# Routing of the first mixture layer: transposes ahead of time, choices taken on logits, and one scatter per choice

## The chip, the cores and the metric

The kernel runs on one core of a Trainium2 chip. The metric is the device time of one execution in microseconds (us), as the median of several executions. Engines are named as the profile names them: PE is TensorE, with PEld for its weight loads, DVE is VectorE, ACT is ScalarE, POOL is GpSimd, and SP is SyncE, which here only issues DMAs.

## The reference, cut to what matters

The program is a decoder of four layers on x of shape (8, 256, 128), float32. Each layer has a self-attention, a cross-attention and a feed-forward part, each followed by a residual sum and a layernorm. The change touches the feed-forward part of layer 0, a mixture of 8 experts, and the last steps of the cross-attention ahead of it.

```python
E, TOP_K, D, H, CAPACITY = 8, 2, 128, 512, 256
xf = x.reshape(b * s, d)                      # 2048 tokens of 128
logits = xf @ Wg                              # 2048 x 8
probs = softmax(logits, axis=-1)
vals, idx = top_k(probs, TOP_K)
w = vals / (sum(vals, -1, keepdims=True) + 1e-09)
for k in range(TOP_K):
    oh = one_hot(idx[:, k], E)
    pos = cumsum(oh, axis=0) - 1 + counts[None, :]
    keep = (oh == 1) & (pos < CAPACITY)
    counts = counts + sum(keep, axis=0)       # the second choice queues behind the first
    combine = combine + w[:, k][:, None] * keep
for e in range(E):
    h = gelu(xf @ W1[e] + b1[e])
    out = out + combine[:, e][:, None] * (h @ W2[e] + b2[e])
```

Each token goes to its two best experts, each expert takes at most 256 (token, choice) pairs in order, all first choices ahead of all second choices, and what does not fit is dropped.

## The kernel before, in words

The stages run in the order L0a, L0x, L0f, L1a and so on: the cross-attention L0x is followed by the mixture L0f. Every engine has its own program, written out by hand, and the engines meet in semaphores. `sem.wait_ge(n)` holds an engine, and with it all that stands behind it in its program. Nothing is reordered at run time. x lies in SBUF as `x_tok`, 16 tiles of 128 tokens (two tiles per batch), and the semaphore `x_done` counts batches that have gone through a stage's layernorm.

**The end of L0x.** The stage is a loop over steps g, with 8 steps (PAIRS) per batch. The last scores are computed at g = 63 and the last weighted values at g = 65. For the last batch there follow the copy of the outputs by VectorE (L2401), their turning by TensorE (L1273), the division by VectorE (L2412 to L2418), a transpose (L1289), a copy by ScalarE (L1964), the output projection (L1297), and residual, moments and normalisation by VectorE (L2473, L2242 to L2253), with the inverse root of the variance by GpSimd in between (L630).

**The routing in L0f.** TensorE waits until all eight batches are normalised, transposes the 16 tiles (L1380) into four PSUM banks, and after ScalarE's copies to `QT` (L2015) forms 16 products of 128 tokens by 8 logits (L1386). VectorE subtracts each token's largest logit (L2619, L2620), ScalarE takes the exponentials (L2017), and VectorE works out probabilities and both choices as one-hot rows (`top2`, L2579 to L2589; `w8` holds 8 for expert 0 down to 1 for expert 7 and breaks ties). Four small TensorE products with a triangle and with ones give positions within a tile and counts per tile for both choices (L1394, L1396). VectorE sums the counts over the tiles in four doubling steps (L2632, L2634) and turns choice and position into a row number of a DRAM buffer `x_slots` (8 experts of 256 rows), `slot_of`, for both choices at once (L2638 to L2662). A token that is not kept gets a number beyond the bound, which the DMA skips.

GpSimd fills some constants at the start of L0f (`later_consts`, L615 to L625). Then it waits for `slot_of` and issues 32 indirect DMAs (L804), one per tile and choice, each writing 128 rows of `x_tok` into `x_slots`. SyncE waits for all 32 to land and loads the buffer back (L584). TensorE, ScalarE and VectorE run the experts from there (L1404 to L1425, L2023, L2670, L2674), their results go to `y_slots` (L588), and GpSimd fetches two rows per token with 32 more indirect DMAs (L795) that VectorE weighs and adds (L2687, L2691).

TensorE waits for `later_consts` ahead of the first expert's input. Of these constants the experts read only `SEL`, in L1425.

## Time and profile before

| | us |
|---|---|
| median of 3 runs (2016.09 to 2019.49) | 2016.48 |
| the profiled execution, its own time | 2024.31 |
| its span in the trace | 2022.6 |
| routing, from the first transpose to the first scatter | 298.16 to 323.13 |
| 32 scatters, first start to last start | 323.13 to 363.05 |
| experts, first to last TensorE instruction | 368.33 to about 410 |
| 32 fetches and the final sums | 413.30 to about 465 |

Starts in the trace count from the start of the span. The profiled execution took 7.8 us more than the median of the others. Its own parts are compared with each other. The granted clock of TensorE is given as a share of full speed, 2.4 GHz, so that 0.50 is 1.2 GHz.

### The profile page before, as it was taken

Reading aid. Unit: us, or ns where it says so; the run is one execution under the profiler, and the core shown is the slowest. Engines: PE = TensorE matmul, PEld = TensorE weight load, DVE = VectorE, ACT = ScalarE, POOL = GpSimd, SP = SyncE. Lnnn points to the kernel's source line nnn. Section 1 sums busy time; section 2 is a strip of 40 time slices with the busy share of each in tenths; the row PEclk is TensorE's granted clock in tenths of the full one; section 3 lists DMA queues with packets and bytes.
Section 4 is the critical chain, followed back from the end, with each engine's and each line's share of the span. In section 5 each row is a group of like instructions: output and inputs, shape, how many; then the busy total and the mean of one; then the engine's idle time right before and its main releaser. Section 6 shows DMA issues by size and latency. Waiting matters only on the chain.

```text
span 2022.6 us, 34313 instructions
## 1 busy us (share of the span) xinstructions
PE 1636.8 (81%) x12460; PEld 1173.2 (58%) x12460; DVE 1373.1 (68%) x3111; ACT 1096.4 (54%) x2271; POOL 697.5 (34%) x773
## 2 busy tenths in 40 slices
PE   6588871737999788879898889988989987888864
PEld 5344431625777655567777767765559964555532
DVE  2577752137777699567999767759964456478876
ACT  4488850205777477538788345546764441147642
POOL 1344434167888302234665512220000020001238
PEclk9699975868999999986887899999999998979985
DMA  2200000110000000010000100000000000000000
GB/s 89 101 12 11 6 33 36 41 36 18 2 1 1 1 1 2 4 37 1 1 1 1 58 1 2 2 11 1 2 1 1 1 17 1 16 1 1 2 1 21
DMA packets 10422, 29.26 MB, mean 14 GB/s; under 512 B 2113, under 2 KB 6663, under 8 KB 9361
## 3 DMA queue, kind: packets, MB, share of 16 engines
q1 hardware_dynamic: 8210, 24.98, 3.5%
q0 software_dynamic: 2048, 2.12, 0.4%
q8 instruction: 101, 1.65, 0.3%
q14 instruction: 63, 0.52, 0.1%
HBM read 23.92 MB, written 5.24 MB: 14 GB/s over the span
## 4 chain that ended last, share of the span: by engine, by line
PE 41%; DVE 19%; POOL 13%; issue 8%; ACT 3%; DMA 0%; POOLq 0%; DVEq 0%; ACTq 0%
PE PS L1117 5%; PE PS L1199 4%; DVE negmax L2370 4%; PE PS L1259 3%; POOL big L738 3%; PE PS L1454 3%; PE PS L1465 3%; DVE V L2864 3%; POOL big L726 2%; POOL big L734 2%; PE PS L1700 2%; PE PS L1281 2%; DVE QS L2430 1%; PE PS L1174 1%; PE PS L1616 1%
## 5 line engine op out<-in xcount | busy, mean ns | idle before, releaser
L1900 ACT ACTIVATE big<-PS 128x1024 f32<-128x1024 f32 (+1 forms) x256 | 248.2, 971 | 135.8 <-PE PS L1210 135.2
L2370 DVE TENSOR_REDUCE negmax<-PS 128x4 f32<-128x1024 f32 x192 | 234.5, 1222 | 46.2 <-PE PS L1199 44.2
L630 POOL TENSOR_TENSOR rstd<-veps,mhalf 128x2 f32<-128x2 f32 x80 | 58.1, 726 | 397.9 <-DVE veps L2248 396.7
L1199 PE MATMUL PS<-KS,QS 32*128 32x256 f32 (+1 forms) x1152 | 134.8, 320 | 48.2 <-DVE negmax L2370 41.9
L1199 PEld LDWEIGHTS PS<-KS,QS 32*128 32x128 f32 x1152 | 86.5, 188 | 124.5 <-DVE negmax L2370 88.5
L1259 PE MATMUL PS<-big,V 128*32 128x256 f32 (+1 forms) x2048 | 134.4, 381 | 0.0
L1210 PE MATMUL PS<-QS,KS 32*128 32x256 f32 (+1 forms) x1152 | 133.1, 318 | 1.4 <-ACT big L1900 1.4
L1956 ACT ACTIVATE KS<-PS,NB,W 128x256 fp32r<-128x256 f32 x160 | 81.6, 561 | 78.3 <-PE PS L1117 49.2
L656 POOL TENSOR_TENSOR res<-resb,XB 128x256 f32<-128x256 f32 x24 | 17.4, 727 | 303.9 <-ACT resb L1970 303.9
L1956 ACT ACTIVATE QS<-PS,NB,W 128x256 fp32r<-128x256 f32 x160 | 81.6, 561 | 40.7 <-PE PS L1117 40.7
L1117 PE MATMUL PS<-xT,W 128*128 128x256 f32 x320 | 90.4, 407 | 13.3 <-ACT xT L1939 11.3
L692 POOL TENSOR_SCALAR KT<-QT 128x1024 f32<-128x1024 f32 x64 | 66.7, 1042 | 90.4 <-DVE QT L2389 71.6
L952 PE MATMUL PS<-OT,W 128*128 128x256 f32 x272 | 74.9, 397 | 26.3 <-ACT QT L1859 26.3
L2389 DVE SCALAR_TENSOR_TENSOR QT<-PS,wint 128x1024 f32<-128x1024 f32 x64 | 77.5, 1220 | 24.3 <-PE PS L1152 24.0
L1255 PE MATMUL PS<-big,V 128*32 128x512 f32 x512 | 72.8, 693 | 24.4 <-ACT big L1922 12.9
L2430 DVE SCALAR_TENSOR_TENSOR QS<-PS,W,QS 128x256 fp32r<-128x256 f32 x160 | 69.6, 477 | 33.6 <-ACT QS L1956 33.5
L1616 PE MATMUL PS<-On,V 128*128 128x128 f32 x512 | 89.2, 347 | 0.0
L2430 DVE SCALAR_TENSOR_TENSOR KS<-PS,W,KS 128x256 fp32r<-128x256 f32 x160 | 69.5, 476 | 28.3 <-ACT KS L1956 28.2
L1616 PEld LDWEIGHTS PS<-On,V 128*128 128x128 f32 x512 | 82.9, 254 | 9.9 <-issue 9.9
L1210 PEld LDWEIGHTS PS<-QS,KS 32*128 32x128 f32 x1152 | 84.2, 186 | 5.8 <-issue 4.0
L2038 ACT ACTIVATE QT<-PS,W 128x256 f32<-128x256 f32 x128 | 53.7, 471 | 60.0 <-PE PS L1454 60.0
L1600 PE MATMUL PS<-OT,SEL 16*128 16x256 f32 x256 | 74.3, 436 | 13.7 <-DVE V L2868 13.6
(412 smaller groups left out, 4530.5 us busy)
## 6 DMA issues: line engine op xcount, KB each, us to landing
W<-in_wpack SPq DMA_DIRECT2D x1, 4180.0 KB, 13.6
W<-in_wpack SPq DMA_DIRECT2D x1, 2836.5 KB, 9.2
W<-in_wpack SPq DMA_DIRECT2D x1, 2560.0 KB, 8.6
W<-in_wpack SPq DMA_DIRECT2D x3, 772.0 KB, 5.2
mask_i<-in_mask SPq DMA_DIRECT2D x8, 256.0 KB, 2.7
W<-in_wpack SPq DMA_DIRECT2D x1, 1798.0 KB, 6.9
x_tok<-in_x SPq DMA_DIRECT2D x1, 1024.0 KB, 4.9
ctxT<-in_ctx SPq DMA_DIRECT2D x1, 1024.0 KB, 7.7
```

The costliest lines, as they stand in the source:

```text
L952: mm = nc.tensor.matmul(PS[:, QKB[u % 2], k * S:(k + 1) * S], w(f"{n}_w{x}", h * P, (h + 1) * P), OT[:, b, :], start=True, stop=True)
L1117: mm = nc.tensor.matmul(o, w(f"{n}_spread" if a.rope else f"{n}_w{x}", (t0 + t) * P, (t0 + t + 1) * P), rhs, start=True, stop=not masked)
L1199: mm = nc.tensor.matmul(PS[:, MAXB[half], o], QS[r, bm % 2, tm, j * P:(j + 1) * P], KS[r, bm % 2, tm, k], start=not a.causal, stop=last)
L1210: mm = nc.tensor.matmul(PS[:, exp_banks(ge)[half], o], KS[r, be % 2, te, kb * P:(kb + 1) * P], QS[r, be % 2, te, q], start=not a.causal, s ...
L1259: mm = nc.tensor.matmul(out_rows[:, skip:S], v, PX[:, T % 2, h, kb * S:(kb + 1) * S - skip], start=first, stop=last)
L1600: mm = nc.tensor.matmul(PS[:, CB + k // 2, (k % 2) * S:(k % 2 + 1) * S], SEL[:, 4 * c + k, :], C_rows(b), start=True, stop=True)
L1616: mm = nc.tensor.matmul(PS[:, YB, j * P:(j + 1) * P], chunk("h", t)[:, at:at + P], by_state[:, 4 * c + k, :], start=False, stop=c == 3 and ...
L1900: nc.scalar.activation(PX[:, T % 2, 2 * p:2 * p + 2, 0:cols], PS[:, exp_banks(g)[0]:exp_banks(g)[0] + 2, 0:cols], ACT.Exp, scale=a.scale). ...
L1956: ins = nc.scalar.activation(dst[:, b % 2, t0 + t, :], PS[:, bank, t * S:(t + 1) * S], ACT.Identity, bias=NB[:, "qk".index(x), t0 + t:t0 + ...
L2370: ins = nc.vector.tensor_reduce(negmax[:, h:h + 2, :].rearrange("p h j -> p (h j)"), banks.rearrange("p h (j k) -> p (h j) k", j=2), AX.X, ...
L2389: nc.vector.scalar_tensor_tensor(clipped(QT, g), PS[:, pair_banks(g):pair_banks(g) + 2, :], -100.0 / a.scale, capT[:, g // PAIRS % 2, :].u ...
L2430: ins = nc.vector.scalar_tensor_tensor(to, PS[:, bank, t * S:(t + 1) * S], w(f"{n}_b{x}", t0 + t, t0 + t + 1), to.bitcast(F32), ALU.add, A ...
```

## The change

The first 14 of the 16 transposes move into the last steps of L0x, between instructions of the last batch, and ScalarE's copies with them. The bank of each tile is `logit_bank(t)`. The last two tiles are transposed in L0f, and then all 16 products with the router's weights follow. VectorE takes each choice on the logits and not on the probabilities: first choice, its positions (`slots(0)`) with one scan over the tiles' counts in place of the doubling steps, `slot_of` for k = 0, and then the same for the second choice. GpSimd issues 16 scatters of the first choice as soon as they are numbered, then the 16 of the second, and `later_consts` follows behind them. The wait for these constants on TensorE moves to the first expert's second layer. The zero fill of `fetched` moves from the start of VectorE's part to the end of the routing. The triangle `tri` now counts what comes behind a token in its tile, with minus signs, and the scan's sum includes the tile.

```diff
-            nc.gpsimd.memset(tri[:, :], 1.0).then_inc(consts, 1)
+            nc.gpsimd.memset(tri[:, :], -1.0).then_inc(consts, 1)
...
-                pool.wait_ge(sem(f"{n}_slots"), 2)
                 pool.wait_ge(sem(f"{n}_cleared"), 16)
-                for t in range(NT):
-                    for k in range(2):
+                for k in range(2):
+                    pool.wait_ge(sem(f"{n}_slots"), 2 * k + 2)
+                    for t in range(NT):
                         nc.gpsimd.indirect_dma_start(x_slots, ...
+                later_consts()
                 pool.wait_ge(sem(f"{n}_stored"), 16 * E)
...
                 if s == "L0f":
-                    later_consts()
                     L0f()
...
+                        if g == PAIRS * B + 2:
+                            logit_turns(0, 4)
+                        elif g == PAIRS * B + 4:
+                            logit_turns(4, 8)
+                            logit_turns(8, 12)
+                        elif g == PAIRS * B + 6:
+                            logit_turns(12, 14)
                         outputs_of(0)
...
+            def logit_turns(a, b):
+                pe.wait_ge(*x_ready("L0f", (b - 1) // 2))
+                for t in range(a, b):
+                    mm = nc.tensor.transpose(PS[:, logit_bank(t), (t % 4) * P:(t % 4 + 1) * P], x_tok[:, t, :], ident)
+                mm.then_inc(sem("L0f_lg_psum"), 1)
+
+            def logits(a, b):
+                pe.wait_ge(*loaded("L0f"))
+                pe.wait_ge(sem("L0f_lg"), {4: 1, 8: 2, 12: 3, 14: 4, 16: 5}[b])
+                for t in range(a, b):
+                    mm = nc.tensor.matmul(PS[:, 4, t * E:(t + 1) * E], QT[...], w("L0f_wg"), start=True, stop=True)
...
             def L0f():
                 n = "L0f"
-                pe.wait_ge(*loaded(n))
-                pe.wait_ge(x_done, base[n])
-                for c in range(4):
-                    for k in range(4):
-                        mm = nc.tensor.transpose(PS[:, c, k * P:(k + 1) * P], x_tok[:, 4 * c + k, :], ident)
...
+                logit_turns(2 * B - 2, 2 * B)
+                logits(0, 4)
+                logits(4, 8)
+                logits(8, 12)
+                logits(12, 14)
+                logits(14, 16)
                 for k in range(2):
+                    pe.wait_ge(sem(f"{n}_slots"), 2 * k + 1)
...
-                pe.wait_ge(consts, CONSTS)
                 turn_slots(0)
...
+                    if a.clip and g == PAIRS * B + 3:
+                        logit_copy(0, 4, 1)
+                    elif a.clip and g == PAIRS * B + 5:
+                        logit_copy(4, 8, 2)
+                        logit_copy(8, 12, 3)
...
+                def choose(k, of):
+                    ch.step(nc.vector.tensor_tensor(found, of, wide(rts[:, k, :]), ALU.is_equal))
+                    ch.step(nc.vector.tensor_tensor(found, found, w8, ALU.mult))
+                    ch.step(nc.vector.tensor_reduce(row8[:, k, :], found, AX.X, ALU.max))
+                    nc.vector.tensor_tensor(ohb[:, k, :, :], found, wide(row8[:, k, :]), ALU.is_equal)\
+                      .then_inc(sem(f"{n}_slots"), 1)
+
+                def slots(k):
+                    dve.wait_ge(sem(f"{n}_counts"), k + 1)
+                    ch.step(nc.vector.tensor_copy(by_expert(cnt), PS[:, 1, ...]))
+                    if k:
+                        ch.step(nc.vector.tensor_tensor(... full, ALU.add))
+                    ch.step(nc.vector.tensor_tensor_scan(pre, keep_on, cnt, 0.0, ALU.mult, ALU.add))
+                    ch.step(nc.vector.tensor_tensor(pos, PS[:, 0, ...], by_tile(pre), ALU.add))
+                    ch.step(nc.vector.tensor_tensor(pos, pos, ohb[:, k, :, :], ALU.mult))
+                    ch.step(nc.vector.tensor_reduce(place[:, k, :], pos, AX.X, ALU.add))
+                    ch.step(nc.vector.tensor_scalar(kept[:, k, :], ...))
+                    ch.step(nc.vector.scalar_tensor_tensor(place[:, k, :], row8[:, k, :], ...))
+                    ch.step(nc.vector.scalar_tensor_tensor(place[:, k, :], kept[:, k, :], ...))
+                    nc.vector.tensor_scalar(slot_of[:, k, :], ...).then_inc(sem(f"{n}_slots"), 1)
...
+                choose(0, logits)
+                nc.vector.tensor_tensor(rt[:, 0, :, :], logits, wide(rts[:, 0, :]), ALU.subtract)\
+                  .then_inc(sem("logits_shifted"), 1)
+                dve.wait_ge(sem(f"{n}_slots"), 1)
+                ch.step(nc.vector.scalar_tensor_tensor(rest, ohb[:, 0, :, :], -BIG, logits, ALU.mult, ALU.add))
+                ch.step(nc.vector.tensor_reduce(rts[:, 1, :], rest, AX.X, ALU.max))
+                slots(0)
+                choose(1, rest)
...
+                slots(1)
...
+                line.did(nc.vector.memset(fetched[:, :, :, :], 0.0))
```

In the fences below a line is a group of equal instructions on one engine, with its line number, its operation, output and inputs, the output's size and the count. The first shows TensorE from the last values of L0x to the counts of the routing, before:

```order
L1255 MATMUL PS<-big,V 32x512 x16
L1273 MATMUL PS<-W,OT 128x72 x8
L1289 MATMUL PS<-W,On 128x128 x2
L1297 MATMUL PS<-W,xs 128x128 x2
L1380 MATMUL PS<-W,x_tok 128x128 x16
L1386 MATMUL PS<-W,QT 128x8 x16
L1394 MATMUL PS<-ohb,tri 128x128
L1396 MATMUL PS<-ohb,onesb 128x128
```

And now, in the same place (L1388 are the transposes, L1395 the products with the router's weights):

```order
L1259 MATMUL PS<-big,V 32x512 x16
L1388 MATMUL PS<-W,x_tok 128x128 x4
L1277 MATMUL PS<-W,OT 128x72 x8
L1388 MATMUL PS<-W,x_tok 128x128 x8
L1293 MATMUL PS<-W,On 128x128 x2
L1388 MATMUL PS<-W,x_tok 128x128 x2
L1301 MATMUL PS<-W,xs 128x128 x2
L1388 MATMUL PS<-W,x_tok 128x128 x2
L1395 MATMUL PS<-W,QT 128x8 x16
L1412 MATMUL PS<-ohb,tri 128x128
```

Four transposes stand ahead of the turning of the last outputs, eight behind it, two behind the last transpose of L0x, and two are left behind the last projection. All 16 products remain where they were.

GpSimd between the last inverse root of L0x and the first fetch, before:

```order
L630 TENSOR_TENSOR rstd<-veps,mhalf 128x2
L615 MEMSET SEL 16x2048
L616 MEMSET causal 128x512
L617 MEMSET causalT 128x128
L619 AFFINE_SELECT SEL<-SEL 16x2048
L622 AFFINE_SELECT causal<-causal 128x512
L625 AFFINE_SELECT causalT<-causalT 128x128
L804 DMA x_slots<-x_tok,slot_of 2048x128 x32
L795 DMA big<-y_slots,slot_of 128x128 x12
```

And now:

```order
L634 TENSOR_TENSOR rstd<-veps,mhalf 128x2
L808 DMA x_slots<-x_tok,slot_of 2048x128 x32
L619 MEMSET SEL 16x2048
L620 MEMSET causal 128x512
L621 MEMSET causalT 128x128
L623 AFFINE_SELECT SEL<-SEL 16x2048
L626 AFFINE_SELECT causal<-causal 128x512
L629 AFFINE_SELECT causalT<-causalT 128x128
L799 DMA big<-y_slots,slot_of 128x128 x12
```

The six instructions of `later_consts` stand behind the scatters, and nothing of GpSimd stands between the last inverse root and the first scatter.

VectorE from the first look at the logits to the first choice's slot numbers, now (before, 39 rows stand from there to the slot numbers of both choices):

```order
L2689 TENSOR_REDUCE rts<-PS 128x16
L2661 TENSOR_TENSOR rt<-PS,rts 128x128
L2662 TENSOR_TENSOR rt<-rt,W 128x128
L2663 TENSOR_REDUCE rt<-rt 128x16
L2664 TENSOR_TENSOR ohb<-rt 128x128
L2691 TENSOR_TENSOR rt<-PS,rts 128x128
L2694 SCALAR_TENSOR_TENSOR rt<-ohb,PS 128x128
L2695 TENSOR_REDUCE rts<-rt 128x16
L2669 COPY big<-PS 128x128
L2672 SCALAR_TENSOR_TENSOR big<-big 128x128
L2673 TENSOR_TENSOR big<-PS,big 128x128
L2675 TENSOR_TENSOR big<-big,ohb 128x128
```

L2672 is the scan. Behind these stand a reduction (L2676), three operations on 16 numbers per partition (L2677 to L2680) and L2682, which writes `slot_of`, 17 instructions in all. The second choice, the weights and the zero fill follow.

## Rows read from the trace of the kernel before

**Rows 1.** The page: the chain that ended last, share of the span by engine.
```profile
PE 41%; DVE 19%; POOL 13%; issue 8%; ACT 3%; DMA 0%; POOLq 0%; DVEq 0%; ACTq 0%
```

**Rows 2.** Stretches, all engines: busy us (instructions), granted clock, DMA share, GB/s.
```profile
290.00:298.00 8.00, 1.91 (x6) 1.22 (x6) 4.43 (x11) 0.37 (x1) 2.59 (x3) 0.53 0.00 0
298.10:308.50 10.40, 10.27 (x48) 10.21 (x48) 3.50 (x2) 2.35 (x4) 3.44 (x5) 0.50 0.65 252
323.00:365.00 42.00, 0.00 (x0) 0.00 (x0) 0.32 (x3) 0.00 (x0) 31.44 (x32) 0.50 0.07 25
```

**Rows 3.** Chain of waits, 363 to 370 us: start, length, what.
```profile
363.05 2.14 DMA x_slots<-x_tok,slot_of
...
365.20 2.99 DMA big<-x_slots
```

**Rows 4.** Timeline of TensorE: start, length, instruction, idle before and releaser.
```profile
287.37 2.00 PE L1273 MATMUL PS<-W,OT 128*128 128x72 f32 x16 [0.86 <-DVE OT L2401]
291.38 0.69 PE L1289 MATMUL PS<-W,On 128*128 128x128 f32 x2 [2.01 <-DVE On L2418]
292.53 1.23 PE L1297 MATMUL PS<-W,xs 128*128 128x128 f32 x4 [0.46 <-ACT xs L1964]
298.16 3.65 PE L1380 MATMUL PS<-W,x_tok 128*128 128x128 f32 x16 [4.41 <-DVE x_tok L2253]
301.60 6.83 PE L1386 MATMUL PS<-W,QT 128*128 128x8 f32 x32
...
374.73 1.06 PE L1423 MATMUL PS<-W,QT 128*128 128x128 f32 x8
```

**Rows 5.** Timeline of VectorE in the routing.
```profile
308.47 0.29 DVE L2619 TENSOR_REDUCE rts<-PS 128x16 f32<-128x128 f32 x1 [6.01 <-PE PS L1386]
...
310.07 0.29 DVE L2581 TENSOR_TENSOR rt<-rt,rts 128x128 f32<-128x128 f32 x1
310.40 0.29 DVE L2583 TENSOR_REDUCE rts<-rt 128x16 f32<-128x128 f32 x1
...
314.96 0.42 DVE L2629 COPY big<-PS 128x256 f32<-128x256 f32 x1 [0.70 <-PE PS L1396]
...
322.05 0.18 DVE L2662 CAST slot_of<-rt 128x32 int32<-128x32 f32 x1
```

**Rows 6.** Timeline of GpSimd, constants and first scatters.
```profile
296.07 1.80 POOL L615 MEMSET SEL<- 16x2048 f32 x1
...
301.68 0.29 POOL L625 TENSOR_SCALAR_AFFINE_SELECT causalT<-causalT 128x128 bf16<-128x128 bf16 x1
323.13 1.25 POOL L804 DMA_INDIRECT x_slots<-x_tok,slot_of  x1 [21.15 <-DVE slot_of L2662]
324.68 0.99 POOL L804 DMA_INDIRECT x_slots<-x_tok,slot_of  x1 [0.31 <-issue]
```

**Rows 7.** VectorE's last normalisation in L0x, on the timeline.
```profile
296.15 1.86 DVE L2253 TENSOR_SCALAR x_tok<-res,mv,rstd 128x128 f32<-128x128 f32 x2 [0.82 <-POOL rstd L630]
```

**Rows 8.** Line L2253 up to 300 us: durations ns minimum/median/maximum.
```profile
L2253 DVE TENSOR_SCALAR x_tok<-res,mv,rstd x16: 334/341/1798, 137.3 to 296.4; 128x128 f32<-128x128 f32 x16
```

**Rows 9.** Scatters and fetches: durations ns minimum/median/maximum, first and last start.
```profile
L804 POOL DMA_INDIRECT x_slots<-x_tok,slot_of x32: 972/974/1246, 323.1 to 363.0; - x32
```
```profile
L795 POOL DMA_INDIRECT big<-y_slots,slot_of x32: 996/1007/1070, 413.3 to 457.5; - x32
```

**Rows 10.** VectorE groups by shape: busy us, mean ns; idle before.
```profile
L2864 DVE TENSOR_TENSOR_SCAN V<-big 128x1024 f32<-128x1024 f32 x32 | 74.8, 2338 | 0.6 <-PE PS L1616 0.6
...
L2615 DVE MEMSET big<- 128x4096 f32 x1 | 3.5, 3472 | 1.0 <-issue 1.0
```

**Rows 11.** Stretches again: the experts, and a busy stretch of a later stage.
```profile
372.00:411.00 39.00, 38.19 (x232) 32.38 (x230) 5.95 (x14) 12.56 (x32) 0.00 (x0) 0.99 0.08 25
...
920.00:940.00 20.00, 20.00 (x72) 15.66 (x73) 17.27 (x19) 14.71 (x44) 12.91 (x6) 0.59 0.00 1
```

**Rows 12.** Timeline of ScalarE: the last copy of L0x.
```profile
292.11 0.37 ACT L1964 COPY xs<-PS 128x256 f32<-128x256 f32 x1 [8.93 <-PE PS L1289]
```

More of the change, by code:

```diff
@@ L2630, in L0f @@
-                a, b = cnt, pre
-                for d in (1, 2, 4, 8):
-                    ch.did(nc.vector.tensor_copy(b[:, :, 0:d, :], a[:, :, 0:d, :]))
-                    for k in range(2):
-                        ch.did(nc.vector.tensor_tensor(b[:, k, d:NT, :], a[:, k, d:NT, :], a[:, k, 0:NT - d, :], ALU.add))
-                    ch.wait()
-                    a, b = b, a
-                ch.step(nc.vector.tensor_scalar(big[:, 512:520], a[:, 0, NT - 1, :], float(CAPACITY), None, ALU.min))
@@ L2647, in L0f @@
-                kept = big[:, 1024:1280].rearrange("p (k t e) -> p k t e", k=2, t=NT)
-                first_of = w("w8").unsqueeze(1).broadcast_to([P, NT, E])
-                one_hot = rt[:, 2:4, :, :]
-                ch.step(nc.vector.tensor_scalar(big[:, 1024:1280], big[:, 768:1024], float(CAPACITY), None, ALU.is_le))
-                for k in range(2):
-                    ch.did(nc.vector.scalar_tensor_tensor(pos[:, k, :, :], first_of, -float(CAPACITY), pos[:, k, :, :],
-                                                          ALU.mult, ALU.add))
@@ L2660, in L0f @@
-                ch.step(nc.vector.scalar_tensor_tensor(place_of, keep_of, -2.0 * E * CAPACITY, place_of, ALU.mult, ALU.add))
-                ch.step(nc.vector.tensor_scalar(place_of, place_of, float(E * CAPACITY - 1 + 2 * E * CAPACITY), None, ALU.add))
-                nc.vector.tensor_copy(slot_of[:, :, :].rearrange("p k t -> p (k t)"), place_of).then_inc(sem(f"{n}_slots"), 1)
+                w8 = w("w8").unsqueeze(1).broadcast_to([P, NT, E])
+                found, rest, prob, scaled = (rt[:, k, :, :] for k in (5, 2, 1, 3))
@@ new lines, in L0f, with by_expert, by_tile @@
+                kept, place, row8 = (rt[:, 4, k:k + 4, :].rearrange("p a b -> p (a b)").rearrange("p (k t) -> p k t", k=2)
+                                     for k in (0, 4, 8))
+                cnt, pre = big[:, 0:128], big[:, 128:256]
+                pos = big[:, 256:384].rearrange("p (t e) -> p t e", t=NT)
+                keep_on, full = big[:, 384:512], big[:, 512:520].unsqueeze(2)
+                def by_expert(t):
+                    return t.rearrange("p (e t) -> p e t", e=E)
+                def by_tile(t):
+                    return t.rearrange("p (e t) -> p t e", e=E)
@@ new lines, in L0f @@
+                ch.step(nc.vector.scalar_tensor_tensor(rest, ohb[:, 0, :, :], -BIG, logits, ALU.mult, ALU.add))
+                ch.step(nc.vector.tensor_reduce(rts[:, 1, :], rest, AX.X, ALU.max))
+                slots(0)
+                choose(1, rest)
+                dve.wait_ge(sem("logits_exp"), {"L0f": 1, "L2f": 2}[n])
+                ch.did(nc.vector.tensor_scalar(full[:, :, 0], by_expert(pre)[:, :, NT - 1], float(CAPACITY), None, ALU.min))
+                ch.step(nc.vector.tensor_reduce(rts[:, 0, :], prob, AX.X, ALU.add))
```

82 lines of the change are left out of this document (40 added, 42 removed).

## The prediction, as it stood before the changed kernel had run

> **What bounds the kernel now.** I read the page's chain first: it is spread over TensorE, VectorE and GpSimd [rows 1], so no engine bounds the whole and the stage at hand has to be read by itself. The table of stretches shows that stage. From 323 to 365 us TensorE and ScalarE do nothing, VectorE 0.32 us, and GpSimd issues 32 scatters; before that TensorE is busy with the logits for 10.27 of 10.40 us, at the granted clock 0.50, which is 1.2 GHz [rows 2]. The chain of waits then says how the stage hangs together: the last scatter's issue and landing (363.05, 2.14 us), the load of the buffer (365.20), and the experts behind it [rows 3]. The timelines give the way up to the first scatter. It is one line without a branch: normalisation of the last batch, 16 transposes at 298.16, 16 products at 301.60 [rows 4], VectorE from 308.47 to the cast of `slot_of` at 322.05 + 0.18 = 322.23 [rows 5], first scatter at 323.13 [rows 6]. So whatever shortens this line starts the scatters earlier by as much, and as each later step waits only for the one before, the rest of the program too. The 32 scatters themselves (323.13 to 363.05, 39.9 us) have no one who could be overtaken: a pitch of 1.28 us, of which 0.97 is the instruction and 0.30 its issue [rows 3, 6, 9].
>
> **Normalisation of the last batch (L2253).** Its two instructions took 1.86 us [rows 7], where one takes 0.34 in the median, 0.68 for two, and 1.80 at most [rows 8]. Beside them GpSimd filled `SEL`, 296.07 to 297.87 [rows 6]: the outlier ends with that fill. The change puts the fill behind the scatters, so nothing of GpSimd lies there any more. Bounds: 0 if the slow one had another cause, 1.86 - 0.68 = 1.2 us if it was this. No other work of the trace in that place would explain it, so I take 1.2 gained. The Trainium skill (SBUF — State Buffer, Who interferes with whom) states that VectorE and GpSimd share a pair of ports which one instruction holds until it ends, and names `tensor_scalar` among those of VectorE that may want it. The row agrees, and the 1.2 us does not depend on it.
>
> **Transposes and products.** 16 transposes took 3.65 us, 0.228 each, and the first product started 301.60 - 298.16 = 3.44 us behind the first of them [rows 4]. Two remain on the path, 0.46 us, and the products follow at once, as the copies of the first twelve tiles are long done and ScalarE has the time of 14 products for the other two. That is 3.0 us gained. The 16 products, 6.83 us, stay whole on the path: the change moves only transposes and copies, and TensorE's wait for the last batch stands ahead of the first product, in spite of the idle time of 4.41 us ahead of it [rows 4].
>
> What the 14 moved ones cost in L0x: four have the 0.86 us of idle time ahead of L1273 (they need 0.91 at the low clock), eight the 2.01 us ahead of L1289 (1.82), two the 0.46 us ahead of L1297 (0.46) [rows 4]. ScalarE gets three copies of 512 columns, of which the last ends shortly before the copy at 292.11 that is on the path [rows 12]. Everything just fits. If nothing overlapped it would be all of 14 x 0.228 = 3.2 us, if all did it is 0. Three gaps as wide as their filling speak for the lower end, and I take 0.2 lost.
>
> **VectorE, from the first reduction to the slot numbers.** Before: 308.47 to 322.23, 13.76 us for both choices, with one wait for ScalarE's exponentials and one of 0.70 us for TensorE's four count products [rows 5]. Now 17 instructions stand ahead of the first choice's numbers. Ten of them work on 128 numbers per partition and hold the next one up: a pitch of 310.40 - 310.07 = 0.33 us, 3.3 us. Two of that size (the one-hot row and the subtraction for the exponentials) do not hold each other, about 0.45 together. Three on 16 numbers cost 0.18 [rows 5] and the gap of 0.04, 0.65 together, and the last one 0.18. The scan is not in this stage before. Its nearest row is 2.34 us for 1024 numbers, an eighth of which is 0.29 [rows 10]. Below it can't be less than any operation on 128 numbers, 0.29; above it is 2.34. I take an eighth plus a fixed part of some 0.15, 0.45 us. The sum is 3.3 + 0.45 + 0.65 + 0.18 + 0.45 = 5.0 us, and 8.8 us are gained. The wait for the counts is covered: the one-hot row is done 1.6 us in, the answer takes up to 0.70, and VectorE reaches the copy of the counts at 2.4 us. If TensorE is slower it is 0.3 at most. The exponentials are off this part altogether.
>
> **The second choice.** Its numbers are due when 16 scatters have been issued, 20.4 us behind the first. VectorE has 16 instructions up to them, under 5 us, so there is no wait between scatters 16 and 17; 15 us of cover would have to go first. Then come the weights, about 3 us, and the fill of `fetched`, 3.47 us [rows 10], all beside the scatters and long before the experts' first copy.
>
> **The scatters** stay 32 and go one after the other. New is that VectorE works beside the first nine or so (some 5 + 3 + 3.5 us over 1.28 us). The first scatter before, with VectorE at work, took 1.25 us, and the next came 1.55 us behind it and not 1.28 [rows 6]: if that was VectorE and not a first issue's own cost, nine of them lose 9 x 0.27 = 2.4 us. The fetches, with VectorE at work between them throughout, take 1.007 against 0.974 us [rows 9], 9 x 0.03 = 0.3 us. They are 32 cases against one: I take 0.3 lost. The first issue's extra is paid in both kernels. A gain in issue time has nothing it could come from.
>
> **Constants.** `later_consts` takes from 296.07 to 301.97, 5.9 us [rows 6], and starts when the last scatter is issued, at about 351.3 in the new time, so it ends at 357.2. The first second layer, at 374.73 before [rows 4], is due at 362.0. Cover 4.8 us, cost nothing; beyond that each microsecond counts in full. The fetches stand behind the constants, but wait for the stores 40 us later.
>
> **The sum** against the profiled execution: 1.2 + 3.0 + 8.8 - 0.2 - 0.3 = 12.5 us gained, 2024.31 to 2011.8. That execution lies 7.8 us above the median of the runs, 2016.48; the parts it is made of don't say where, so I carry the difference over: 2016.48 - 12.5 = 2004.0 us.
>
> **The rivals.**
>
> The clock stays up (a). If the moved transposes keep TensorE at 2.4 GHz, the two transposes and 16 products halve: 7.3 / 2 = 3.6 us more, 2000.4. For it: the clock was between its levels at 290 to 298 (0.53) with 1.91 us busy, and ten transposes more go in just there. Against it: the idle time of over 4 us ahead of the stage remains, and an almost unbroken stream of 10.40 us stayed at 0.50 to its end [rows 2]. The Trainium skill (TensorE: Matmul & The Clock Gate, What's actually happening) has the clock follow how busy the engine was; by it that stream ought to have risen to the full clock, and the row shows that it did not. By the rule the time would be nearer 2000.4, by the row 2004.0.
>
> L0x ends later (b). The gaps are as wide as what goes in, and a late copy on ScalarE would hold the one at 292.11. Half of the 3.2 us and more on ScalarE, 2 us in all: 2006.0.
>
> VectorE holds the scatters back (c). If GpSimd could not issue while VectorE works, the 11.5 us behind the first numbers would go in between: 2004.0 + 11.5 - 0.3 = 2015.2, no change. For it: the 1.25 us of the first scatter, and rows 7, which show one of the two engines held by the other. Against it: the fetches. The Trainium skill (SBUF — State Buffer, SBUF: two separate sides) tells of GpSimd that cannot write the descriptors of its DMAs while VectorE runs an instruction that takes both ports, which speaks for (c) and 2015; rows 9 show 0.03 us of it for each fetch, which speaks for 2004.
>
> TensorE's clock comes up late for the experts (d), the one that ends slower. They run 38.19 us of 39.00 busy at 0.99 [rows 11] and hang on TensorE alone. At 0.50 that would be 38 us more, 2042. It decides from 12.5 us of delay on. For it: a later stage was fully busy for 20 us at 0.59 [rows 11], so a full engine is no warrant. Against it: the idle time ahead of the experts is as long as before, and so is what they run.
>
> **How the numbers follow.** Forecast 0.76, at 2004.0, (a) 0.07, (b) 0.08, (c) 0.05, (d) 0.04. The range: below, the clock, 2000.5. Above, the outlier that was no outlier (1.2), the slower scatters (2.4 in place of 0.3) and L0x's end (2.0 in place of 0.2) hardly fall together: two of them give 2004.0 + 4 = 2008, and the spread of the runs before, 3.4 us for three, adds one: 2009. Below 0.2%, 4 us, a difference cannot be told from none by this measurement. The forecast, (a) and (b) are all beyond it, 0.91. (c) is no change, 0.05, and (d) slower, 0.04.
>
> **What would show it.** The last L2253 pair of L0x takes 0.7 us and not 1.86. The logits take 7.3 us from the first of the last two transposes to VectorE's first reduction, at a clock of 0.50; less at a higher one is (a). From that reduction to the first `slot_of` are 5.0 us, and the scan is 0.45. The first scatter starts 13 us earlier than 323.13, at about 310.1, and all 32 lie at a pitch of 1.28 with no gap in the middle; a pitch of 1.5 or more beside VectorE's work is (c). L1289 starts at 291.4 or little later, else (b). The first L1425 has no wait for GpSimd. The prediction is wrong if the first scatter comes earlier as said and the experts do not.

## The result, and the profile after

| | before | changed |
|---|---|---|
| median, us (fastest to slowest) | 2017.34 (2016.09 to 2019.49) | 2005.55 (2003.50 to 2008.16) |
| the profiled execution, its own time | 2024.31 | 2006.41 |
| its span | 2022.6 | 2004.6 |
| granted clock over the span | 0.889 | 0.892 |

The changed kernel takes 0.9927 of the time (95% interval 0.9898 to 0.9956), 11.8 us less by the medians of four runs each. Forecast were 2004.0 us, with a range of 2000.5 to 2009.0.

The spans differ by 18.0 us. The stage at hand gives 13.9 of them. It is measured between two points that both kernels have: the start of GpSimd's inverse root for the seventh batch of L0x, and that of the last of L0f's. The other 4 us come from stretches whose instructions are the same in both kernels. Two executions of the changed kernel alone differ by 6.9 us by the time the first of those points is reached. Behind the second point the trace before runs for 1558.8 us, that of the changed kernel for 1554.9, and those of the ten experiments, whose instructions there are the same, for 1552.6 to 1559.4. So only the 13.9 us are to be explained.

| piece, us from start to start | before | changed | gained | forecast |
|---|---|---|---|---|
| L0x's tail, seventh to eighth inverse root | 13.68 | 12.92 | 0.76 | -0.2 |
| last normalisation (the pair) | 1.86 | 0.60 | 1.26 | 1.2 |
| its end to VectorE's first reduction | 10.46 | 7.42 | 3.04 | 3.0 |
| first reduction to first scatter | 14.66 | 5.92 | 8.74 | 8.8 |
| first to 32nd scatter | 39.92 | 39.93 | 0 | -0.3 |
| 32nd scatter to experts | 5.28 | 5.03 | 0.25 | 0 |
| experts to first fetch | 44.97 | 45.15 | -0.18 | 0 |
| first fetch to L0f's last inverse root | 50.50 | 50.42 | 0.08 | 0 |

The chain's shares have hardly moved against [rows 1]:

```profile
PE 42%; DVE 20%; POOL 13%; issue 8%; ACT 4%; DMA 0%; POOLq 0%; DVEq 0%; ACTq 0%
```

The stretches answer to [rows 2, 11] (start:end, length, busy us and instructions of PE, PEld, DVE, ACT and POOL, granted clock, DMA share, GB/s):

```profile
290.00:298.00 8.00, 3.57 (x20) 3.08 (x19) 3.21 (x13) 1.76 (x5) 0.70 (x1) 0.73 0.16 41
295.80:303.30 7.50, 7.32 (x34) 7.23 (x34) 0.29 (x4) 0.37 (x1) 0.00 (x0) 0.50 0.89 350
309.00:351.00 42.00, 0.40 (x2) 0.13 (x2) 9.37 (x27) 0.00 (x0) 32.42 (x33) 0.50 0.07 25
358.00:397.00 39.00, 38.13 (x231) 32.31 (x229) 5.95 (x14) 12.56 (x32) 0.00 (x0) 0.99 0.08 25
```

The two last transposes and 16 products fill 7.50 us and not 10.40, still at 0.50. Beside the scatters VectorE now works for 9.37 us and not 0.32. The experts' busy 38.13 of 39 us and their clock are as before.

TensorE's timeline, for [rows 4] (start, length, instruction, idle before it and who ended that):

```profile
286.25 0.94 PE L1388 MATMUL PS<-W,x_tok 128*128 128x128 f32 x4
287.18 2.00 PE L1277 MATMUL PS<-W,OT 128*128 128x72 f32 x16
289.02 1.04 PE L1388 MATMUL PS<-W,x_tok 128*128 128x128 f32 x8
291.19 0.44 PE L1293 MATMUL PS<-W,On 128*128 128x128 f32 x2 [1.13 <-DVE On L2446]
...
292.09 0.71 PE L1301 MATMUL PS<-W,xs 128*128 128x128 f32 x4 [0.24 <-ACT xs L1983]
295.86 0.69 PE L1388 MATMUL PS<-W,x_tok 128*128 128x128 f32 x2 [3.06 <-DVE x_tok L2281]
296.35 6.84 PE L1395 MATMUL PS<-W,QT 128*128 128x8 f32 x32
...
361.65 0.48 PE L1445 MATMUL PS<-W,SEL 8*128 8x128 f32 x2
```

The moved transposes lie in the gaps meant for them, and eight of them took 1.04 us where 1.82 was reckoned. L1293 and L1301 (L1289 and L1297 before) take 0.44 and 0.71 us where they took 0.69 and 1.23. L1445, the first reader of `SEL`, has no idle time ahead of it.

VectorE, for [rows 5, 7]; L2689 is the first reduction, L2672 the scan, L2682 writes each choice's `slot_of`:

```profile
295.20 0.60 DVE L2281 TENSOR_SCALAR x_tok<-res,mv,rstd 128x128 f32<-128x128 f32 x2 [0.82 <-POOL rstd L634]
...
303.22 0.29 DVE L2689 TENSOR_REDUCE rts<-PS 128x16 f32<-128x128 f32 x1 [7.13 <-PE PS L1395]
...
305.88 0.42 DVE L2672 TENSOR_TENSOR_SCAN big<-big 128x128 f32<-128x128 f32 x1
...
308.01 0.17 DVE L2682 TENSOR_SCALAR slot_of<-rt 128x16 int32<-128x16 f32 x1
...
312.57 0.46 DVE L2682 TENSOR_SCALAR slot_of<-rt 128x16 int32<-128x16 f32 x1
```

From 303.22 to 308.18 are 4.96 us. The second choice is numbered at 313.03, when three scatters have been issued, so nothing waits for it. GpSimd, for [rows 6, 9]:

```profile
309.14 1.32 POOL L808 DMA_INDIRECT x_slots<-x_tok,slot_of  x1 [13.97 <-DVE slot_of L2682]
310.77 0.98 POOL L808 DMA_INDIRECT x_slots<-x_tok,slot_of  x1 [0.31 <-issue]
...
355.49 0.29 POOL L629 TENSOR_SCALAR_AFFINE_SELECT causalT<-causalT 128x128 bf16<-128x128 bf16 x1
```
```profile
L808 POOL DMA_INDIRECT x_slots<-x_tok,slot_of x32: 971/972/1323, 309.1 to 349.1; - x32
```

The median scatter took 972 ns beside VectorE's work as before without it (974). The constants are complete at 355.78, 5.9 us ahead of their reader. The chain, for [rows 3]:

```profile
349.07 2.13 DMA x_slots<-x_tok,slot_of
...
351.22 2.84 DMA big<-x_slots
```

### The profile page after: what moved, and what is told of

Same layout as the page of the kernel before. It is cut to its first block, busy times and chain, and to the rows that moved or that the text cites. A ratio compares the mean times of both kernels' runs of the same rounds, so it can differ in the third digit from the quotient of the medians.

```text
span 2004.6 us, 34311 instructions
## 1 busy us (share of the span) xinstructions
PE 1633.3 (81%) x12457; PEld 1169.0 (58%) x12460; DVE 1369.6 (68%) x3107; ACT 1096.5 (55%) x2272; POOL 698.4 (35%) x773
## 4 chain that ended last, share of the span: by engine, by line
PE 42%; DVE 20%; POOL 13%; issue 8%; ACT 4%; DMA 0%; POOLq 0%; DVEq 0%; ACTq 0%
PE PS L1121 5%; PE PS L1203 4%; DVE negmax L2398 4%; PE PS L1263 3%; POOL big L742 3%; PE PS L1473 3%; PE PS L1484 3%; POOL big L730 3%; DVE V L2909 2%; POOL big L738 2%; PE PS L1277 2%; PE PS L1719 2%; PE PS L1285 2%; DVE QS L2458 1%; PE PS L1178 1%
## 5 line engine op out<-in xcount | busy, mean ns | idle before, releaser
L1259 PE MATMUL PS<-big,V 128*32 128x512 f32 x512 | 72.8, 693 | 24.4 <-ACT big L1941 12.9
L730 POOL TENSOR_SCALAR big<-big,rsum 128x256 f32<-128x256 f32 (+1 forms) x144 | 60.3, 432 | 71.5 <-DVE rsum L2331 71.5
L1635 PE MATMUL PS<-On,V 128*128 128x128 f32 x512 | 84.8, 335 | 0.0
```

Source lines behind the costliest of these rows:

```text
L730: ins = nc.gpsimd.tensor_scalar(PRW[:, u % 4, c0:c1], PRW[:, u % 4, c0:c1], rsum[:, u % 16, j:j + 1], 1.0, ALU.mult, ALU.mult)
L1635: mm = nc.tensor.matmul(PS[:, YB, j * P:(j + 1) * P], chunk("h", t)[:, at:at + P], by_state[:, 4 * c + k, :], start=False, stop=c == 3 and ...
```

## The experiments

Pieces are read from each kernel's profile, as in the table above. "Way" is the stretch from the eighth inverse root (that of L0x's last batch) to the first scatter, "experts" that from their first instruction on TensorE to the first fetch, "stage" the whole between the two fixed points.

| | ratio to before (95% interval) | tail | way | experts | stage |
|---|---|---|---|---|---|
| before | | 13.68 | 27.72 | 44.97 | 182.07 |
| changed kernel | 0.9927 (0.9898 to 0.9956) | 12.92 | 14.68 | 45.15 | 168.13 |
| again | 0.9898 (0.9858 to 0.9938) | 13.55 | 14.68 | 45.55 | 169.00 |
| constants first | 0.9929 (0.9899 to 0.9958) | 13.55 | 15.94 | 44.81 | 169.84 |
| other form | one run | 13.23 | 14.69 | 44.76 | 168.26 |
| transposes back | 0.9923 (0.9898 to 0.9947) | 15.68 | 14.56 | 46.10 | 171.97 |
| one wait | 0.9926 (0.9894 to 0.9958) | 13.56 | 19.24 | 44.95 | 173.09 |
| products early | 0.9901 (0.9884 to 0.9918) | 12.93 | 10.35 | 45.55 | 164.30 |
| warm experts | 0.9931 (0.9914 to 0.9947) | 12.95 | 14.68 | 45.04 | 168.26 |
| warm logits | 0.9931 (0.9913 to 0.9948) | 12.39 | 11.49 | 46.08 | 165.50 |
| combined | 0.9917 (0.9902 to 0.9932) | 13.55 | 9.92 | 44.28 | 163.40 |
| warm, landed | 0.9930 (0.9914 to 0.9945) | 13.56 | 14.68 | 43.65 | 167.53 |

The intervals overlap: a difference of 1 to 5 us between two of these kernels isn't told apart by their times, and is read from the pieces.

**The changed kernel again**, unchanged, run beside constants first, transposes back and one wait.

> The changed kernel once more, unchanged. Theory: the gain is the earlier first scatter and nothing else. In the trace of the first profile the stage gave 13.9 us (GpSimd's first inverse root behind the mixture stood at 428.77 before and at 414.73 after, less the 0.19 us by which the whole trace after starts earlier), so the first scatter again starts within 0.1 us of 309.1, and the runs come out 12 to 15 us below those of the kernel before. Rival: the further 3.9 us that the first profile shows in later stages (18.0 us of span in all) belong to the change as well; then the runs come out about 18 us below, and the same places of the trace (the later steps of the second layer) are again earlier by 1.3 and 1.4 us.

It took 2002.3 us against 2018.79, 16.5 us less, which lies between the theory's 12 to 15 and the rival's 18. The profile decides: the stage gave 13.1 us, and the rest behind it took 1556.7 us, inside the spread of all the kernels. The way repeats to 0.01 us; the tail doesn't (12.92 and 13.55).

**Constants first.** Edit:

```
+                later_consts()
                 for k in range(2):
                     pool.wait_ge(sem(f"{n}_slots"), 2 * k + 2)
...
-                later_consts()
```

> GpSimd's constants back ahead of the scatters, all else as changed. Theory: VectorE's last normalisation of L0x is held by GpSimd's fill of SEL. The pair of L2253 takes about 1.86 us again in place of 0.60, and all that follows starts 1.26 us later: first scatter at about 310.4. GpSimd has the constants done at about 301, long before the first slot numbers, so nothing else is delayed. Rival: the slow pair before was a chance of that execution, and the constants' place is worth nothing: pair 0.6 us, first scatter at 309.1.

2007.91 us. The pair is back at 1.86 us and the way longer by 1.26, with the fill of `SEL` beside it. VectorE, then GpSimd:

```profile
290.22 1.86 DVE L2281 TENSOR_SCALAR x_tok<-res,mv,rstd 128x128 f32<-128x128 f32 x2 [0.82 <-POOL rstd L634]
```
```profile
290.14 1.79 POOL L619 MEMSET SEL<- 16x2048 f32 x1
```

That the fill causes it is shown. Whether it is the form of VectorE's instruction was asked with **other form**: the same order, and the last batch normalised by another instruction of the same arithmetic (a single run, 2004.92 us).

```
+                    if s == "L0x" and i == B - 1:
+                        ins = nc.vector.scalar_tensor_tensor(x_tok[...], res[:, j, :], mv[:, j, 0:1],
+                                   rstd[:, j:j + 1].broadcast_to([P, P]), ALU.subtract, ALU.mult)
```

> GpSimd's constants ahead of the scatters as in the first of these experiments, but the last normalisation of L0x written as scalar_tensor_tensor, which takes the inverse root as a second input from SBUF and not as a scalar; elsewhere in this kernel that form takes 0.34 us, as the other does. Theory: it is the form of the tensor_scalar on VectorE that cannot run beside GpSimd's fill, not the fill alone (the Trainium skill, SBUF — State Buffer, Who interferes with whom, lets an instruction with two SBUF inputs run beside one of GpSimd that only writes). Then the pair takes 0.6 to 0.7 us in spite of the fill, and the first scatter stands 14.7 us behind the inverse root. Rival: any instruction of VectorE on SBUF waits for the fill: pair 1.86 us, first scatter 15.9 us behind.

```profile
292.89 0.61 DVE L2282 SCALAR_TENSOR_TENSOR x_tok<-res,mv,rstd 128x128 f32<-128x128 f32 x2 [0.82 <-POOL rstd L634]
```
```profile
292.81 1.79 POOL L619 MEMSET SEL<- 16x2048 f32 x1
```

Under the same fill this form isn't held: 0.61 us, and the way is 14.69 us as in the changed kernel. The 1.2 us could have been had without moving the constants. The Trainium skill (SBUF — State Buffer, Who interferes with whom) names `tensor_scalar` among the forms that can take the ports shared with GpSimd, and has an instruction with two SBUF inputs held only by a GpSimd instruction that reads SBUF, which a fill doesn't do. Both rows agree.

**Transposes back.** All 16 transposes and their copies in L0f again:

```
-                        if g == PAIRS * B + 2:
-                            logit_turns(0, 4)
...
-                logit_turns(2 * B - 2, 2 * B)
+                pe.wait_ge(x_done, base[n])
+                logit_turns(0, 4)
...
+                logit_turns(14, 16)
```

> The 14 transposes and ScalarE's copies back behind the last normalisation, all else as changed. Theory: 14 transposes of 0.23 us cost 3.0 us on the path, and without them in the last steps of L0x the clock falls to 0.6 in 290 to 292 us again, so that the last transpose and projection of L0x take 0.8 us longer in all: first scatter at 309.1 + 3.0 + 0.8 = 312.9. Rival: the 0.8 us in the end of L0x came from somewhere else (a luckier clock in that execution): clock 1.00 in 290 to 292 here too, and first scatter at 312.1.

2005.94 us, 3.6 above the changed kernel again, and the stage longer by 2.97 us. But the pieces fell otherwise than the theory said: the way did not grow (14.56), and the tail did, by 2.1 us. TensorE's timeline, and the clock in the routing:

```profile
283.90 3.69 PE L1277 MATMUL PS<-W,OT 128*128 128x72 f32 x16 [0.86 <-DVE OT L2425]
289.60 0.69 PE L1293 MATMUL PS<-W,On 128*128 128x128 f32 x2 [2.01 <-DVE On L2442]
290.75 1.22 PE L1301 MATMUL PS<-W,xs 128*128 128x128 f32 x4 [0.46 <-ACT xs L1981]
295.03 3.52 PE L1381 MATMUL PS<-W,x_tok 128*128 128x128 f32 x16 [3.06 <-DVE x_tok L2277]
298.38 3.85 PE L1388 MATMUL PS<-W,QT 128*128 128x8 f32 x32
```
```profile
296.00:298.00 2.00, 2.00 (x11) 2.00 (x10) 0.00 (x0) 1.28 (x3) 0.00 (x0) 0.50 0.83 266
298.00:300.00 2.00, 2.00 (x20) 2.00 (x18) 0.00 (x0) 1.02 (x3) 0.00 (x0) 0.94 1.14 492
```

Here the clock came up behind 3 us of transposes, and the products took 3.85 us and not 6.84. In the kernel before the same sequence stayed at 0.50 for 10.4 us [rows 2]. One execution of each: what decides between them these runs don't show. So this run doesn't confirm the 3.0 us of the transposes, which rest on the two timelines at 0.50 alone; in the way of this execution their old place cost nothing. The theory's 0.8 us in L0x did come: L1293 and L1301 took 0.69 and 1.22 us again, as before the change. The rest of the longer tail is L1277, 3.69 us at the low clock against 2.00 to 2.36 us in the other kernels.

**One wait.** GpSimd waits for both choices ahead of the first scatter:

```
-                    pool.wait_ge(sem(f"{n}_slots"), 2 * k + 2)
+                    pool.wait_ge(sem(f"{n}_slots"), 4)
```

> The first scatter waits for the slot numbers of both choices, all else as changed. Theory: VectorE needs 4.8 us from the first numbers to the second (308.18 to 313.03), of which 0.3 us were a wait on GpSimd's own scatter, so that the first scatter comes at 309.14 + 4.5 = 313.7; no further loss, and every later step 4.5 us later. Rival: scattering beside VectorE's work costs something that this saves (the first scatter took 1.32 us and not 0.97, and the second came 1.63 us behind it): then the first scatter takes 0.97 and the loss is 4.2 or less.

2008.96 us; the way grows by 4.56 us, what the second choice's numbers need, and is lost whole. The first scatters:

```profile
307.61 1.25 POOL L808 DMA_INDIRECT x_slots<-x_tok,slot_of  x1 [18.54 <-DVE slot_of L2682]
309.16 0.98 POOL L808 DMA_INDIRECT x_slots<-x_tok,slot_of  x1 [0.31 <-issue]
```

1.25 us, the second 1.55 us behind it, as before, and 39.84 us from the first to the last of the 32. The ten profiles with the overlap have 39.92 to 40.08. The overlap thus costs 0.1 to 0.24 us and brings 4.56.

**Products early.** Eight products go behind the last projection of L0x and four ahead of the last two transposes, where TensorE waits for the last normalisation:

```
+                        elif g == PAIRS * B + 7:
+                            logits(0, 4)
+                            logits(4, 8)
...
-                logit_turns(2 * B - 2, 2 * B)
-                logits(0, 4)
-                logits(4, 8)
                 logits(8, 12)
+                logit_turns(2 * B - 2, 2 * B)
```

> Twelve of the 16 products with the router's weights ahead of the last two transposes: eight right behind the last projection of L0x, four at the start of the routing, all else as changed. Theory: TensorE stands idle for 3.06 us between the last projection and the last two transposes, and the 16 products (6.84 us) are bound by TensorE alone, so that they end 3.1 us earlier: VectorE's first reduction 13.9 us behind GpSimd's inverse root of L0x's last batch less what now stands before it, that is first scatter 11.6 us behind that inverse root and not 14.7. Rival: the last two transposes, now behind twelve products, come so late that the wait for ScalarE's copy of them (0.9 us) is no longer covered; then the gain is 2.2 us.

```profile
290.62 4.16 PE L1398 MATMUL PS<-W,QT 128*128 128x8 f32 x24
294.63 0.67 PE L1391 MATMUL PS<-W,x_tok 128*128 128x128 f32 x2
295.09 1.75 PE L1398 MATMUL PS<-W,QT 128*128 128x8 f32 x8
```

An fp32 product of this kind is two records, so the first line is 12 products. They took 4.16 us, the first of them at a granted clock of 0.92 (stretch 290 to 292), the rest at 0.50. The last two transposes start 0.84 us after the end of the last normalisation (293.79), for which TensorE then no longer waited. Only these and four products are left. The way is shorter by 4.33 us, more than the 3.1 of the theory; about 1.0 us of that is the faster start, as 12 of the 16 products at 0.50 would take 5.13 us (12/16 of 6.84). The clock, with TensorE busy throughout:

```profile
290.00:292.00 2.00, 1.92 (x16) 1.93 (x16) 1.00 (x4) 0.30 (x2) 0.00 (x0) 0.92 0.00 0
292.00:294.00 2.00, 2.00 (x12) 2.00 (x11) 1.08 (x6) 0.00 (x0) 0.70 (x1) 0.50 0.00 0
```

It fell, at 291.7, although the idle time ahead of the products was gone. That is 12.2 us behind the seventh inverse root, the same point at which it fell in the changed kernel, where TensorE stood idle. The runs: 1998.63 us (1994.85 to 2002.25) against 2016.61. It is the fastest median of all, and by its pieces it beats the changed kernel by 3.8 us, by its ratio not certainly.

**Warm logits.** Nine products of ones, whose result nobody reads, behind the end of L0x, to hold the clock:

```
+                        elif g == PAIRS * B + 8:
+                            warm(6, 9)
...
+            def warm(bank, times):
+                for _ in range(times):
+                    nc.tensor.matmul(PS[:, bank, 0:P], onesf[:, :], onesf[:, :], ...)
```

> Nine products of ones by ones, 128 x 128 float32, that nothing reads, between the last projection of L0x and the last two transposes, all else as changed. Theory: the logits run at 1.2 GHz because TensorE stood idle for 3.06 us before them. With the idle time filled the last two transposes and the 16 products take half of 7.36 us: first scatter 11.2 us behind the inverse root of L0x's last batch and not 14.7. Rival: products with 8 columns do not hold the clock up, whatever stood before them; then it falls while they run and the gain is 1.5 us or less, and the filling costs up to 0.8 us where it runs into the transposes.

```profile
284.60 2.17 PE L1390 MATMUL PS<-onesf 128*128 128x128 f32 x18
287.82 0.44 PE L1395 MATMUL PS<-W,x_tok 128*128 128x128 f32 x2 [1.05 <-DVE x_tok L2288]
288.09 3.86 PE L1402 MATMUL PS<-W,QT 128*128 128x8 f32 x32
```
```profile
288.00:290.00 2.00, 2.00 (x20) 2.00 (x20) 0.04 (x1) 0.37 (x1) 0.00 (x0) 1.00 0.74 174
```

The way is 3.19 us shorter: rival (a) is a real mechanism, worth this much. That the changed kernel lacks it only because TensorE stands idle for 3.06 us ahead of the logits is not shown. Products early fills the same time with products of 8 columns, and the clock falls all the same; here 2.17 us of products of 128 columns fill it, 1.05 us stay idle, and the clock holds. So it is not the idle time alone; with one execution of each kernel, what else decides stays open. The runs: 2001.77 us.

**Warm experts.** Sixteen such products ahead of the experts, released by GpSimd behind its 30th scatter:

```
+                        if k == 1 and t == NT - 3:
+                            pool.sem_inc(sem(f"{n}_nearly"), 1)
...
+                pe.wait_ge(sem(f"{n}_nearly"), 1)
+                warm(7, 16)
```

> Sixteen products of ones by ones, 128 x 128 float32, that nothing reads, on TensorE from the issue of the 30th scatter on, all else as changed. Theory: the experts' first 4 us run at 1.2 GHz only because TensorE stood idle before them. With the clock up at the start the first 16 records of the first layers (5.30 us) and the first transposes take half: GpSimd's first inverse root behind the mixture comes 2 us nearer to the first scatter (103.6 us and not 105.6). Rival: the clock falls again in the gap between these products and the load's landing, or the first experts wait for VectorE and ScalarE anyway: no gain; if the products run beyond the landing, up to 1 us lost.

```profile
330.62 6.52 PE L1390 MATMUL PS<-onesf 128*128 128x128 f32 x32 [22.56 <-POOLq L812]
352.56 1.12 PE L1429 MATMUL PS<-W,big 128*128 128x128 f32 x4 [15.42 <-DMA big<-x_slots]
```

No test: the release came at 330.5, 14.4 us before the 30th scatter started (344.87), since the increment ran in GpSimd's queue while the scatters ahead of it still stood in line, and TensorE's clock was down again (5.18 us for the first 16 records of the experts' first layers). The runs: 2003.16 us. So it was asked once more, with **warm, landed**: release when all scatters have landed.

```
+                pe.wait_ge(sem(f"{n}_scattered"), 16 * 2 * NT)
+                warm(7, 7)
```

> Seven products of ones by ones, 128 x 128 float32, that nothing reads, on TensorE from the landing of the last scatter on, all else as changed. In the version before this one they ran too early: TensorE stood idle for 15.4 us between them and the experts, since GpSimd gave the signal long before its scatters were issued. Theory: now they fill the 2.9 us between the landing and the load, the clock rises up to 3 us earlier, and the experts (45.0 to 45.6 us from the first transpose to the first fetch) take 43 to 44. Rival: the clock's rise does not follow the start of the work alone, so that it gains in one execution and not in the next, 0 to 2 us.

```profile
346.00 3.36 PE L1388 MATMUL PS<-onesf 128*128 128x128 f32 x14 [41.45 <-DMA x_slots<-x_tok,slot_of]
...
350.30 3.85 PE L1435 MATMUL PS<-On,W 128*128 128x256 f32 x16
```

The first 16 records of the experts' first layers take 3.85 us where the changed kernel takes 5.30. The ones (3.36 us) are a little longer than the load (2.71 to 2.99 us in before, changed kernel and repeat), and TensorE goes from them to the experts without a pause: from the last scatter's start to the experts are 5.33 us, against 4.91 to 5.28 in the kernels without ones there. The experts take 43.65 us, against 44.76 to 46.10; from that start to the first fetch that leaves 49.0 us against 49.8 to 51.3. In the time of the runs (2003.2 us) it doesn't show.

**Combined.** Products early, two warming products at three places between them, and those ahead of the experts:

```
+                        elif g == PAIRS * B + 7:
+                            logits(0, 4)
+                            warm(6, 2)
+                            logits(4, 8)
...
+                warm(6, 2)
                 logits(8, 12)
+                warm(6, 2)
+                logit_turns(2 * B - 2, 2 * B)
```

> The changed kernel with twelve of the 16 products ahead of the last two transposes, six products of ones by ones (128 x 128 float32, that nothing reads) between them, and seven more when all scatters have landed. Theory: the 1.2 GHz products leave 3.09 us between the last normalisation and VectorE's first reduction; with the clock held up that is 0.15 for the start, 0.23 for two transposes, 0.6 for ScalarE's copy of them and 0.45 for the last products, so 1.4 to 1.8 us, and the first scatter stands 9.0 us behind the inverse root of L0x's last batch (14.68 in the changed kernel, 10.35 with early products alone). The experts start warm and give 1 to 2 us more. In all 6 to 8 us less than the changed kernel. Rival: six products are too few to hold the clock beside those with 8 columns; then it is 10.3 to 11.0 us to the first scatter, no better than early products alone, and the gain is that of early products, 4.3 us.

The shortest stage, 163.40 us, with a way of 9.92, between the theory's 9.0 and the rival's 10.3. The six ones did hold the clock, but they also kept TensorE busy: it starts the last two transposes 0.85 us after the end of the last normalisation (292.98), where the theory had 0.15. These take 0.38 us and not 0.69, and of the four products behind them the last two meet a wait of 0.21 us for ScalarE's copy and a clock that falls to 0.50 at 295:

```profile
293.83 0.38 PE L1397 MATMUL PS<-W,x_tok 128*128 128x128 f32 x2
...
294.77 0.81 PE L1404 MATMUL PS<-W,QT 128*128 128x8 f32 x4 [0.21 <-ACT QT L2047]
```

Its stage is 4.7 and 5.6 us shorter than the two of the changed kernel, where 6 to 8 were forecast. Its time, 2002.01 us, ratio 0.9917, is no better than that of products early alone (0.9901): 0.9 us in the stage is below what these runs resolve.

## Why the prediction was right

**The normalisation** was forecast at 1.2 us and gave 1.26. The fill as its cause is shown by moving it back, and the form of the instruction as the condition by the other form.

**The transposes**: forecast 3.0, measured 3.04. Right in this kernel, where the clock stayed at 0.50 as [rows 2] had said. In transposes back the clock rose and the way did not grow, so that the size of this term hung on a clock that the prediction could read off one execution only.

**VectorE**: 5.0 forecast, 4.96 measured, with the scan at 0.42 us and the next instruction 0.46 behind it, where 0.45 was taken from the row of 1024 numbers. The 8.7 us are two effects that one wait tells apart: the second choice lies beside the scatters (4.56 us) and the rest, 4.2 us, is the shorter work on each choice (logits in place of probabilities, one scan in place of four steps, no wait for the exponentials), whose parts no run separates.

**The scatters**: the term "I take 0.3 lost" was mis-sized. From the first to the 32nd it is 0 here and at most 0.16 us (40.08 against 39.92) in the other profiles. What stood against (c) was right in its result, but not in its reading: the prediction has VectorE at work beside the fetches throughout, and charges 0.03 us of each to it [rows 9]. Before the change VectorE was idle for 8.98 us up to L2687 at 419.64, and the fetches in that time took as long:

```profile
413.30 1.06 POOL L795 DMA_INDIRECT big<-y_slots,slot_of  x1 [49.28 <-DMA y_slots<-V]
414.67 1.01 POOL L795 DMA_INDIRECT big<-y_slots,slot_of  x1 [0.30 <-issue]
```

So the 0.03 us are not VectorE's, and a first issue has an extra of its own even beside an idle VectorE (1.06 us against 1.00 to 1.01). Whether all of the 0.27 us in [rows 6] is of this kind is not shown, as VectorE works beside the first scatter in one wait too (1.25 us, and 1.55 to the second). It is not a price of every scatter beside VectorE: in the changed kernel the first took 1.32 us, the second came 1.63 us behind it, and from the third on all keep 0.97 and 0.30.

**L0x's tail** had the wrong sign: "I take 0.2 lost" was a gain of 0.76 us, in the repeat of 0.13. The sum counted what the moved transposes occupy and at the low clock, not what they do for their neighbours. TensorE had work in the gaps, and its clock was higher behind them. Before, then changed:

```profile
290.00:292.00 2.00, 0.62 (x2) 0.29 (x2) 1.25 (x3) 0.00 (x0) 0.00 (x0) 0.62 0.00 0
292.00:294.00 2.00, 1.29 (x5) 0.93 (x4) 0.21 (x1) 0.37 (x1) 0.00 (x0) 0.50 0.00 0
```
```profile
290.00:292.00 2.00, 0.72 (x5) 0.42 (x4) 1.07 (x3) 1.07 (x4) 0.00 (x0) 1.00 0.00 0
292.00:294.00 2.00, 0.71 (x4) 0.52 (x4) 0.98 (x4) 0.32 (x2) 0.00 (x0) 0.92 0.00 0
```

Rival (a) put this mechanism on the wrong piece. It held up to L1301, and then the clock fell again, at 293.7, in the idle time ahead of the logits.

The whole gain lies behind the start of L1293 (L1289 before). That instruction starts 9.65 us behind the seventh inverse root in both kernels, so the twelve transposes ahead of it cost nothing. From its start to the eighth inverse root are 4.03 us before and in transposes back, and 3.26 to 3.28 in all ten profiles with the transposes in the tail: 0.75 to 0.77 us less, each time. What differs from one execution to the next lies ahead of it (9.12 to 10.29 us in those ten, 9.65 and 11.65 in the two others), and there the transposes' part can't be told: in transposes back L1277 ran at 0.50 (3.69 us), before it ran at the full clock without any transposes (2.00 us).

**The constants** cost nothing, as said, with 5.9 us of cover (4.8 forecast). **Rival (d)** did not occur: the experts ran at 0.99. **The sum**: 12.5 forecast against 13.9 and 13.1 us in two profiles of the stage; outside the tail 13.2 and 12.9, against 12.7. The forecast's time also rested on carrying the profiled execution's 7.8 us over to the median. The stage can't settle that. By the medians the change gave 11.8 us in this comparison and 16.5 in the repeat, so that a time within 1.6 us of the forecast is in part luck.

**Left open**: why the same 16 transposes and 16 products stayed at 0.50 before and did not in transposes back, and so what the transposes' new place is worth in the mean of many executions.

## What to carry to other kernels

Split what is waited for at the point where its first half is usable: with issues of 1.28 us each in line, half of the numbers bought the whole time of the other half. Before an instruction is moved off the path because another engine seems to hold it, try another form of it. Where TensorE alternates short work and waits, price a moved instruction twice, once for its own time and once for what its presence does to the clock of the next.

## What the runs showed of the hardware

- The 16 products of 128x8 took 6.84 us where the clock stood at 0.50 when they began, and 3.86 us where it stood at 1.00. In the changed kernel and in that before, a stream of transposes and these products, with no idle time to speak of, did not raise the clock in 7.5 and 10.4 us. Nor did they keep it up in products early, where it fell from 1.00 to 0.50 at 291.7, 1.1 us into an unbroken stream of them. In warm logits, behind nine products of 128 columns, a raised clock lasted almost through all 16 (0.84 in the last stretch, 290 to 292).
- GpSimd's indirect DMAs can hold an instruction of VectorE as its fill does. The second write of `slot_of`, at 312.57, ended with the scatter beside it (312.06 + 0.97 = 313.03) and took 0.46 us and not 0.17. The same in six of the ten profiles in which a scatter runs beside it; in the other four it took 0.17 us at the same place, and the fourth scatter, which starts behind it, took 1.05 us in place of 0.97. What decides between the two these runs don't show.

```profile
312.06 0.97 POOL L808 DMA_INDIRECT x_slots<-x_tok,slot_of  x1 [0.30 <-issue]
```

- GpSimd's queue runs ahead of its indirect DMAs. The last of the moves that go with the 32 scatters (duration, first and last start) starts 15.6 us before the last scatter:

```profile
L808 POOLq MOVE  x32: 29/29/29, 308.3 to 333.5; - x32
```
